# The high parts of the summed weights: kept in on-chip memory, or streamed from DRAM with the low parts

## The reference

```python
scale = cond @ norm_w.T + 1.0
ms = jnp.mean(x * x, axis=-1, keepdims=True)
h = x * (scale[:, None, :] * jax.lax.rsqrt(ms + EPS))
u = h @ up_w.T
val, gate = jnp.split(u, 2, axis=-1)
h = val * jax.nn.gelu(gate, approximate=False)
hq = act_quant(h)          # int8 steps by the row's largest value
wq = weight_quant(down_w)  # -1, 0, 1 by the mean of all
y = hq @ wq.T
return y + x
```

## Time and profile before

| | us |
|---|---|
| median of 3 runs | 759.24 (759.22 to 759.32) |
| the profiled execution's own time | 759.19 |
| its span in the trace | 757.4 |
| PE busy | 737.0 (97%) |
| DVE busy | 546.7 (72%) |
| ACT busy | 345.7 (46%) |
| POOL busy | 98.9 (13%) |
| DMA | 116.63 MB, mean 154 GB/s |

### The profile page before, as it was taken

The page is one execution under the profiler, slowest core; times in us unless marked ns, Lnnn a source line. Parts: engine busy times, 40 slices in busy tenths (PEclk is TensorE's granted clock), DMA queues, the critical chain, the costliest instruction groups (busy, mean ns, idle before and its releaser), DMA issues.

```text
span 757.4 us, 15715 instructions
## 1 busy us (share of the span) xinstructions
PE 737.0 (97%) x6218; PEld 610.5 (81%) x6218; DVE 546.7 (72%) x1066; ACT 345.7 (46%) x674; POOL 98.9 (13%) x137
## 2 busy tenths in 40 slices
PE   3999999999999999999999999999999999999998
PEld 2888889888578887888778887788878887688864
DVE  5467777888788775878667775777758776377747
ACT  5789756443254432553235442444325342233425
POOL 2211376763413000000000000000000000000000
PEclk9999999999999999999999999999999999999999
DMA  9877673756645444343533434343443333453302
GB/s 324 285 259 241 189 264 123 229 178 223 200 135 183 153 153 148 116 140 99 183 117 116 130 116 163 108 152 122 125 160 103 98 98 117 128 170 98 103 29 84
DMA packets 43929, 116.63 MB, mean 154 GB/s; under 512 B 4944, under 2 KB 5200, under 8 KB 42704
## 3 DMA queue, kind: packets, MB, share of 16 engines
q1 hardware_dynamic: 43856, 115.63, 47.6%
HBM read 98.83 MB, written 16.78 MB: 153 GB/s over the span
## 4 chain that ended last, share of the span: by engine, by line
PE 86%; DVE 5%; ACT 3%; issue 3%; DMA 1%; POOL 0%; SPq 0%; DVEq 0%; ACTq 0%
PE ps_v L525 16%; PE ps_v L526 15%; PE ps_v L527 15%; PE ps_y L626 12%; PE ps_g L526 8%; PE ps_g L525 8%; PE ps_g L527 8%; PE ps_v L690 1%; DMA sums<-in_up_t_dram 1%; DMA h<-in_x_rows_dram 1%; ACT g L733 1%; ACT w_hi L776 1%; DVE h L1053 0%; PE ps_m L609 0%; DVE xt L1004 0%
## 5 line engine op out<-in xcount | busy, mean ns | idle before, releaser
L525 PE MATMUL ps_v<-x_hi,w_hi 128*128 128x256 f16 x1216 | 332.0, 273 | 3.3 <-DVE ps_g L1036 1.3
L527 PE MATMUL ps_v<-x_hi,w_lo 128*128 128x256 f16 x1216 | 331.9, 273 | 0.0
L526 PE MATMUL ps_v<-x_lo,w_hi 128*128 128x256 f16 x1216 | 331.9, 273 | 0.0
L526 PE MATMUL ps_g<-x_lo,w_hi 128*128 128x256 f16 x640 | 174.8, 273 | 0.0
L527 PE MATMUL ps_g<-x_hi,w_lo 128*128 128x256 f16 x640 | 174.8, 273 | 0.0
L525 PE MATMUL ps_g<-x_hi,w_hi 128*128 128x256 f16 x640 | 174.8, 273 | 0.0
L715 ACT COPY ps_g<-ps_v 128x256 f32<-128x256 f32 x96 | 34.3, 357 | 230.7 <-PE ps_v L527 230.7
L525 PEld LDWEIGHTS ps_v<-x_hi,w_hi 128*128 128x128 f16 x1216 | 119.1, 98 | 21.4 <-DVE ps_g L1036 2.7
L526 PEld LDWEIGHTS ps_v<-x_lo,w_hi 128*128 128x128 f16 x1216 | 119.1, 98 | 15.7
L527 PEld LDWEIGHTS ps_v<-x_hi,w_lo 128*128 128x128 f16 x1216 | 119.1, 98 | 13.9
L726 ACT ACTIVATE g<-ps_g,w_unscale 128x512 f32<-128x512 f32 x128 | 87.3, 682 | 68.1 <-PE ps_g L527 68.0
(11 more groups left out here) (113 smaller groups left out, 581.7 us busy)
## 6 DMA issues: line engine op xcount, KB each, us to landing
w_lo<-w_lo_dram SPq DMA_DIRECT2D x96, 448.0 KB, 3.3
q<-in_up_t_dram SPq DMA_DIRECT2D x16, 512.0 KB, 5.1
xt<-in_x_cols_dram SPq DMA_DIRECT2D x8, 1024.0 KB, 5.2
res<-in_x_rows_dram SPq DMA_DIRECT2D x26, 256.0 KB, 3.6
out_dram<-res SPq DMA_DIRECT2D x26, 256.0 KB, 2.9
sums<-in_up_t_dram SPq DMA_DIRECT2D x12, 512.0 KB, 4.7
xs<-in_x_rows_dram SPq DMA_DIRECT2D x22, 256.0 KB, 3.8
w_lo_dram<-w_lo SPq DMA_DIRECT2D x16, 256.0 KB, 4.8
```

The source lines that it names most:

```text
L525: pe.matmul(to, w_hi[:, wh:wh + P], hi, start=start and kt == 0, stop=False, skip_group_check=True)
L526: pe.matmul(to, w_hi[:, wh:wh + P], lo, start=False, stop=False, skip_group_check=True)
L527: last = pe.matmul(to, w_lo[:, wl:wl + P], hi, start=False, stop=(kt == 1), skip_group_check=True)
```

## The change

The high parts of the four summed operands no longer stay in `w_hi`. ACT writes the high part beside the low part into an output tile of 2048 fp16 a partition (`sum_tile`: for even k the new tile `sum_out`, for odd k both halves of `xs`), DVE writes the low part before it, and one store takes both to DRAM: 512 KB for each of 16 sums instead of 256 KB. `WL` grows from 2048 to 3072, so each slot of `w_lo` and each row of `w_lo_dram` holds four loaded low parts, four summed low parts and four summed high parts; the load of a tile from n = 32 on brings 2816 fp16 a partition, 704 KB instead of 448 KB. In `product` a summed operand's high part comes from the slot. `w_hi` keeps the high parts of the loaded operands alone, with no overlap between tiles.

With this the waits move. ACT's `sum_high` no longer waits for PE (`val_ready`) but, from k = 2 on, until the store of sum k - 2 has landed; DVE's `sum_low` loses that wait. PE's `first_pair` loses its wait for `ws_ready`. A sum's weights in places 2 and 3 now lie in the slot of that number in one piece of 1024 float32, where they lay in two pieces of 512 in a pair of slots.

```diff
@@ -59,10 +60,9 @@
     HB = TB // 2
     TT = TB // P
     WJ = 2 * KT * P
-    WO = NOP * 2 * P
     WA = 4 * 2 * P
     WS = 4 * 2 * P
-    WL = WA + WS
+    WL = WA + 2 * WS
     PAD = 2 * P
     XO = NOP * 2 * HB
     PER_B = NB // B
@@ -134,8 +133,7 @@
 
         lo_dram = nc.dram_tensor("w_lo_dram", [J, P, WL], FP16, kind="Internal").ap()
 
-
-        w_hi = sb("w_hi", [P, PAD + J * WO], FP16)
+        w_hi = sb("w_hi", [P, J * WA], FP16)
         w_lo = sb("w_lo", [P, LS * WL], FP16)
         w_unscale = sb("w_unscale", [P, J], F32)
         dw = sb("dw", [P, J * D], BF16)
@@ -143,6 +141,7 @@
 
         xt = sb("xt", [P, KT, TB], F32)
         xs = sb("xs", [P, 2, D], F32)
+        sum_out = sb("sum_out", [P, 2 * WS], FP16)
         res = sb("res", [P, 2, D], F32)
         ta = sb("ta", [P, 2, HB], F32)
         tb = sb("tb", [P, 2, HB], F32)
@@ -322,15 +321,14 @@
 
         def wb(j):
 
-            return PAD + j * WO
+            return j * WA + PAD
 
         def sum_raw(k):
 
             place = SUM_PLACE[k]
             if place < 2:
-                return sums[:, place * WS:(place + 1) * WS].rearrange("p (a n) -> p a n", a=2)
-            slots = w_lo[:].bitcast(F32).rearrange("p (s c) -> p s c", s=LS)
-            return slots[:, 2 * place - 4:2 * place - 2, WA // 2:WL // 2]
+                return sums[:, place * WS:(place + 1) * WS]
+            return w_lo[:, place * WL + WA:(place + 1) * WL].bitcast(F32)
 
         def sum_loads(k):
 
@@ -338,7 +336,7 @@
 
         def sum_tile(k):
 
-            return xs[:, k % 2, :].bitcast(FP16)
+            return sum_out[:] if k % 2 == 0 else xs[:].rearrange("p a n -> p (a n)").bitcast(FP16)
 
         def sum_store(k):
 
@@ -363,7 +361,7 @@
                     sp.wait_ge(ws_ready, user + 1)
                 elif SUM_PLACE[k] < 2:
                     sp.wait_ge(dw_ready, J)
-                sp.dma_start(sum_raw(k), up_t[k].rearrange("p (a n) -> p a n", a=2)).then_inc(sum_loaded[SUM_PLACE[k]], 16)
+                sp.dma_start(sum_raw(k), up_t[k]).then_inc(sum_loaded[SUM_PLACE[k]], 16)
 
             def store_sum(k):
                 stored, _ = sum_store(k)
@@ -378,8 +376,8 @@
                     sp.wait_ge(lo_stored[j % LS], 16 * (j // LS + 1))
                 if in_seven(n):
                     if n < 2 * J + LS:
-                        last = max(k for k in range(J) if SUM_PLACE[k] == 2 + (n % LS) // 2)
-                        sp.wait_ge(ws_ready, last + 1)
+                        if n % LS in (2, 3):
+                            sp.wait_ge(ws_ready, max(k for k in range(J) if SUM_PLACE[k] == n % LS) + 1)
                     if n < 3 * J:
                         stored, count = sum_store(j)
                         sp.wait_ge(stored, count)
@@ -397,7 +395,7 @@
                 if t >= 2:
                     sp.wait_ge(sumsq_ready, TT + t + 1)
                 if c == 4 and i < 2:
-                    stored, count = sum_store(J - 2 + t % 2)
+                    stored, count = sum_store(J - 1)
                     sp.wait_ge(stored, count)
                 sp.dma_start(xs[:, t % 2, :], x_rows[c][:, i * D:(i + 1) * D]).then_inc(xs_loaded[t % 2], 16)
 
@@ -518,12 +516,16 @@
                     pe.wait_ge(x_lo_ready, made_at(b, xop))
                 to = bank[:, half * HB:(half + 1) * HB]
                 for kt in range(2):
-                    wh = wb(j) + (op * 2 + kt) * P
                     wl = (n % LS) * WL + PAD + (op * 2 + kt) * P
+                    if op >= OS3:
+                        w = w_lo[:, wl + WS:wl + WS + P]
+                    else:
+                        wh = wb(j) + (op * 2 + kt) * P
+                        w = w_hi[:, wh:wh + P]
                     xa = x_at(b, xop) + kt * HB
                     hi, lo = x_hi[:, xa:xa + HB], x_lo[:, xa:xa + HB]
-                    pe.matmul(to, w_hi[:, wh:wh + P], hi, start=start and kt == 0, stop=False, skip_group_check=True)
-                    pe.matmul(to, w_hi[:, wh:wh + P], lo, start=False, stop=False, skip_group_check=True)
+                    pe.matmul(to, w, hi, start=start and kt == 0, stop=False, skip_group_check=True)
+                    pe.matmul(to, w, lo, start=False, stop=False, skip_group_check=True)
                     last = pe.matmul(to, w_lo[:, wl:wl + P], hi, start=False, stop=(kt == 1), skip_group_check=True)
                 return last
 
@@ -556,8 +558,6 @@
 
             def first_pair(n):
                 pe.wait_ge(lo_loaded[n % LS], 16 * ((n - J) // LS + 1))
-                if n < 3 * J:
-                    pe.wait_ge(ws_ready, n % J + 1)
                 if n >= NV:
                     pe.wait_ge(h_ready, n - NV + 1)
                 bank = ps_v[:, n % NV, :]
@@ -778,8 +778,12 @@
 
             def sum_high(k):
                 act.wait_ge(s_step, 4 * (k + 1))
-                act.wait_ge(val_ready, J + min(k + 2, J))
-                act.activation(w_hi[:, wb(k) + WA - PAD:wb(k) + WO].rearrange("p (a n) -> p a n", a=2), sum_raw(k), ACT.Copy,
+                if k >= 2:
+                    stored, count = sum_store(k - 2)
+                    act.wait_ge(stored, count)
+                if k == 1:
+                    act.wait_ge(sumsq_ready, 3 * TT)
+                act.activation(sum_tile(k)[:, WS:2 * WS], sum_raw(k), ACT.Copy,
                                scale=w_scale[:, k:k + 1]).then_inc(ws_hi_ready, 1)
 
             def sum_down(k):
@@ -867,7 +871,7 @@
             pool.tensor_copy(ident_top, ident[:]).then_inc(ident_ready, 1)
 
             def sum_weights(k):
-                a21, a22, a11, a12 = [sum_raw(k)[:, i // 2, (i % 2) * 2 * P:(i % 2 + 1) * 2 * P] for i in range(4)]
+                a21, a22, a11, a12 = [sum_raw(k)[:, i * 2 * P:(i + 1) * 2 * P] for i in range(4)]
                 pool.wait_ge(sum_loaded[SUM_PLACE[k]], sum_loads(k) * 16)
                 pool.tensor_tensor(a22, a21, a22, ALU.add).then_inc(s_step, 1)
                 pool.wait_ge(s_step, 4 * k + 1)
@@ -958,13 +962,8 @@
 
             def sum_low(k):
                 dve.wait_ge(ws_hi_ready, k + 1)
-                dve.wait_ge(sumsq_ready, 3 * TT)
-                if k >= 2:
-                    stored, count = sum_store(k - 2)
-                    dve.wait_ge(stored, count)
-                dve.scalar_tensor_tensor(out=sum_tile(k).rearrange("p (a n) -> p a n", a=2), in0=sum_raw(k),
-                                         scalar=w_scale[:, k:k + 1],
-                                         in1=w_hi[:, wb(k) + WA - PAD:wb(k) + WO].rearrange("p (a n) -> p a n", a=2),
+                dve.scalar_tensor_tensor(out=sum_tile(k)[:, 0:WS], in0=sum_raw(k), scalar=w_scale[:, k:k + 1],
+                                         in1=sum_tile(k)[:, WS:2 * WS],
                                          op0=ALU.mult, op1=ALU.subtract).then_inc(ws_ready, 1)
 
             def rsqrt(c):
```

## The result

| | before | after |
|---|---|---|
| median | 759.53 us (758.05 to 761.25, 20 runs) | 763.27 us (760.68 to 766.81, 20 runs) |
| profiled execution | 759.19 us, span 757.4 | 764.99 us, span 763.2 |
| mean granted clock, all executions | 0.999 or more | 0.9985 or more in 11, 0.995 to 0.998 in 9 |

The changed kernel is slower: the ratio is 1.0048, with a 95% interval from 1.0036 to 1.0061. The forecast of 760.4 us and its range up to 762.2 were too low. The 20 executions fall in two groups. The 11 with the full clock have a median of 761.79 us, the 9 with a lower one 764.44.

A forecast was written before the change was run, and what follows sets the result against it. PE, busy 97%, was taken as the bound, except where a DMA, POOL, ACT and DVE decide near 224 to 240 us. +1.5 for the late load and -0.25 gave +1.25 on 759.19: 760.4 us, range 759.0 to 762.2.

The forecast's parts named there:

- the load of the fifteenth sum: Sum weights' load near 224 us, behind 512 KB more in its queue: 1.5 us later, bounds 0.8 to 3.2.
- rival B: Added bytes almost free, or POOL's steps quicker with less DVE beside them (0.3 us): 759.0 to 759.6; chance 0.22.
- Rival C: Fifteenth sum's load also waits for the store ahead to be written to DRAM: up to 3.2 us late, 762.2; chance 0.15.
- the steady part: Block windows with larger operand loads and stores: traffic does not brake PE and loads arrive in time, 0 us.
- ACT's new wait: ACT's `sum_high` for k waiting for the store of k - 2: tightest pair 2 us early, 0 us.
- PE's other source: PE's matmuls reading a summed high part from `w_lo` rather than `w_hi`: same shape, 0 us.
- The sixteenth sum: Next sum, from POOL at 241.2 to ACT at 242.45: slack covers a load 1.5 us late, 0 us.
- rival D: Operand loads late in every block, PE stopping at each block's start: 765 us or later; chance 0.04.
- the small gain: Near 205 us POOL comes later and mostly misses DVE's `sum_low`, so `turn_max` waits less: -0.25 us (0 to -0.27).

The follow-up runs named there:

- e5: Changed kernel with 448 KB operand loads from n = 36 on and 256 KB sum stores from k = 4 on; 761.02 us, ratio 1.0020.
- e6: Changed kernel with 448 KB operand loads from n = 36 on, its 512 KB sum stores kept; 761.56 us, ratio 1.0024.
- e10: Changed kernel with only DVE's rsqrt chain for block 3 moved one iteration later, loads as late as before; 763.13 us, ratio 1.0044.
- e4: Changed kernel with the loads for sums issued ahead of the stores of sums in each SP iteration; 761.57 us, ratio 1.0022.
- e2: Kernel before with the fifteenth sum's weights loaded one iteration earlier; 758.68 us, ratio 0.9985.
- e3: Kernel before with the fifteenth sum's load issued later, behind its iteration's operand load, no byte added; 762.23 us, ratio 1.0036.
- e1: Changed kernel with the fifteenth sum's weights loaded one iteration earlier; 761.32 us, ratio 1.0025.
- e7: Changed kernel with the loads for the fifteenth and sixteenth sums one iteration earlier; 760.46 us, ratio 1.0006.
- e8: Kernel before with the loads for the fifteenth and sixteenth sums and the rsqrt chain moved, loads one iteration earlier, chain one later; 759.08 us, ratio 0.9986.

## Why the prediction was wrong

**Two terms of the sum failed: "the load of the fifteenth sum", by its size, and the granted clock, which the sum left out.** With the pause as measured and the clock at its full level the time is 761.79 us, the median of those 11 executions, still inside the range of 759.0 to 762.2. What takes the median to 763.27 is the clock.

**The load.** Place and chain were right: the load near 224 us, then POOL, ACT, DVE, PE, with nothing later to give the time back. The load was priced 1.5 us longer and came 2.87 us longer. The price for 256 KB came from two means, one of how the operand loads' own landing grows with their size and one of the whole queue, and gave 0.8 us for each of the two additions. For the store that was about right, 0.67 us (e5 to e6). For the operand loads it was 2.05 us (e6 to after), two and a half times the price. Each of these is from one execution a kernel, though e10's load, with the bytes of after, took 8.29 us. Of the 2.05 us the operand load ahead shows 1.1 in its own landing (5.9 us against 4.8). The sum reckoned only with bytes ahead in the queue; the operand load issued behind the sum's load, 3.70 us later and in flight with it, grew too. That it makes up the rest is possible and not shown. The prediction's upper bound for the term was 3.2 us.

PE's pause was to be 2.4 us instead of 0.86. It was 2.99. So 2.13 of the 2.87 us reached PE, where the prediction passed all of the load's delay on. SP issued the load 1.10 us later than before, with PE 1.40 us later there, and POOL's four steps took 3.20 us instead of 3.48. The second is what rival B had named, with 0.3 us.

**Rival C had the better price, and its mechanism is not shown.** It forecast a load up to 3.2 us late and 762.2 us, because the store ahead has to be written out first. With the order turned round the load takes 1.6 us less (e4), but that is what the forecast's own price gives for 512 KB, and 256 KB more in the store cost 0.67 us, less than that price. Most of the addition came from the operand loads, which C did not name. The Trainium skill ("DMA: Bandwidth & Descriptors", Queues, rings and completion order) has a semaphore write land after earlier writes of its engine. The landings agree: in after those of the operand load, the store, the sum's load and the next operand load come in the order of issue, at 230.2, 231.2, 233.6 and 235.1 us. The landings give no price for it. By another rule of the Trainium skill (same page, Anatomy of one DMA), fitted there to DMAs issued from GpSimd and not from SP, the 512 KB would cost an estimated 1.2 us; the runs show 2.87.

**Missed altogether: the granted clock.** The sum treated a pause as lost time at its own length. In the profiled execution it also cost half the clock for some 6 us behind it, and 9 of 20 executions have a lowered mean clock. The groups' medians are 764.44 and 761.79 us, 2.65 apart; the profile has 2.7 us of slow matmuls, less the 0.45 of the gap that went. Of the 2.9 us between the forecast and 763.27, 1.5 is the way from the full-clock median to the median of all. The full-clock median itself is 2.26 above before: 2.13 for the pause, -0.27 for `turn_max`, and 0.4 left, which block 1 would explain.

**Missed as well: block 1.** I looked for ACT's waits for POOL and found two; I did not look at how far DVE stood behind PE near 180 us, where its chain leaves no slack. DVE in after runs later against PE there. L665 on PE is 0.70 us later than before in this execution:

```profile
77.15 0.32 PE L665 MATMUL ps_y<-ident,d_sum 128*128 128x128 f32 x1 [0.68 <-DVE d_sum L1186]
```

```profile
77.85 0.32 PE L665 MATMUL ps_y<-ident,d_sum 128*128 128x128 f32 x1 [0.68 <-DVE d_sum L1185]
```

The `hidden` of DVE that stood at 163.65 stands at 165.35 in after, 1.70 later, so 1.0 us has been added. At 129.17 it was 1.14 later (128.03 before), and the first 512 KB store is issued at 133.6. So 0.44 us of this was there before any added byte moved. The other 0.56 came in the stretch of sums. There POOL waits 0.92 us for a load at 142.11, and ACT 0.77 us for POOL at 146.80. The trace of before has neither wait; e2's, with the bytes of before, has one of 0.82 us of POOL at 139.95 but none of ACT there.

```profile
128.03 0.74 DVE L1053 SCALAR_TENSOR_TENSOR h<-ps_v,w_unscale,g 128x512 f32<-128x512 f32 x1
163.65 0.74 DVE L1053 SCALAR_TENSOR_TENSOR h<-ps_v,w_unscale,g 128x512 f32<-128x512 f32 x1
```

```profile
129.17 0.74 DVE L1052 SCALAR_TENSOR_TENSOR h<-ps_v,w_unscale,g 128x512 f32<-128x512 f32 x1
142.11 0.94 POOL L876 TENSOR_TENSOR w_lo<-w_lo 128x256 f32<-128x256 f32 x1 [0.92 <-DMA w_lo<-in_up_t_dram]
146.80 1.15 ACT L786 ACTIVATE xs<-w_lo,w_scale 128x1024 f16<-128x1024 f32 x1 [0.77 <-POOL w_lo L882]
165.35 0.74 DVE L1052 SCALAR_TENSOR_TENSOR h<-ps_v,w_unscale,g 128x512 f32<-128x512 f32 x1
```

Over the kernels with the chain in its old place the gap is 0, 0.41 and 0.64 us with the bytes of before, and 0.84 to 2.22 with those of after (0.89 in e5 and e6). It follows DVE: counted from L665 on PE, that `hidden` stands 0.56 and 0.66 us later than before in e2 and e3 (gaps 0.41 and 0.64), 1.0 in after (0.97), 1.54 in e1 (1.53) and 2.24 in e7 (2.22). But in e1 and e7, which have the largest gaps, 1.6 and 1.8 us of this stand already at the `hidden` ahead of the first larger store. This is e7's:

```profile
130.79 0.74 DVE L1052 SCALAR_TENSOR_TENSOR h<-ps_v,w_unscale,g 128x512 f32<-128x512 f32 x1
```

From there to the later `hidden` e7 adds 0.5 us and e1 nothing. So the larger stores and loads can have made some 0.5 us of the gap, in seven of the eight traces of the changed kernel and its variants; e2 adds 0.4 without them. No run changed the bytes in that stretch alone. The rest is a spread between executions, of which the last section names a source.

**Right:** the steady part at 0 (88.81 us of PE in 89.00, DMA share 0.53 where 0.55 was forecast, operand loads at a median of 4.3 us where 4.1 was forecast). ACT's new wait at 0: in after ACT was never released by a store, though the stores took 5.2 to 5.4 us at the median (in e4, with the stores behind the loads, it was once, for 0.72 us). PE's other source at 0. The sixteenth sum was covered in after, and was not where PE came earlier (e1). No rival D: no wait of PE for an operand load shows (its one wait for a DMA, 3.9 us at the start, is in before too).

**Right in part by luck: the small gain.** The gap ahead of `turn_max` went from 1.32 to 1.05 us, since `sum_low` took 1.28 us at 206.11 with POOL idle until 207.00, as said. All eight traces of the changed kernel and its variants have 1.05. But the kernel before does not always meet POOL there: e2 and e3, whose edits come later, have 1.06 and 1.09, and e8 1.28.

```profile
208.48 0.63 PE L609 MATMUL ps_m<-ident,h_max 128*128 128x128 f32 x4 [1.06 <-issue]
```

**Two slips of arithmetic** changed nothing: 96 times 256 KB are 25.2 MB in the units used elsewhere, not 24.6; and B's terms, 0.8 - 0.25 - 0.3, give 759.4 us, not 759.6.

## What to carry to other kernels

Price bytes added to a queue at the transfer on which an engine chain without slack waits, with those issued behind it that are in flight with it, and not by the mean rate; here the added 29 MB cost nothing in the last two thirds of the run and, in the profiled execution, 4.4 us at one load (2.13 for the pause and 2.25 for the clock). Then ask what a pause of PE does to its clock: here, in the profiled execution, 2.1 us more of pause brought 2.7 us of slow matmuls with it. When one transfer sets the end of a chain, issue it an iteration earlier before judging a change that adds traffic, and look what the next one of its kind then does.

## What the runs showed of the hardware

- **The clock after a pause.** Two gaps of 1.94 and 1.05 us, with 0.8 us of work between them, were followed by a granted clock of 0.50 for some 6 us. Over the kernels, with both gaps and the executions with a lowered clock: 1.94 + 1.05 (after, 9 of 20), 1.84 + 1.05 (e10, 5 of 5), 1.61 + 1.05 (e3, 3 of 8, the traced one at full clock); 0.19 + 1.05 (e4, 0 of 8), 0.23 + 1.05 (e6, 0 of 11), 0.86 (before, 0 of 20). One gap of 2.22 us near 180 us was followed by it too (e7, 1 of 12). e1 (2 of 11) and e5 (1 of 11) have such executions without a trace of them; the largest gaps in their traces, past the start, are 1.53 and 1.05 us. The same kernel does it in some executions and not in others. Whether their pauses differed is not known, and no run tells why.
- **Slow matmuls at the start.** In every profile PE's first 128x256 matmuls, from 15.5 to 16.7 us on, are as slow as those behind the pause, 0.42 us each and 0.21 us apart, though the granted clock of these windows reads 1.00 in before and after. The last slow one starts between 18.50 us (e6) and 20.87 us (e4), without order by kernel: 19.04 in before, 20.83 in after. DVE's L965 stood 0.34 us earlier in after than in before at 19.4 us, and 0.72 later at 25.0 (25.73), so the 0.70 us by which the two profiles differ at 77 us came in that stretch.
- **Small DVE operations beside POOL.** The 128x4 operations of the chain take 0.16 us, or 0.57 for many of those that begin while a POOL operation runs; in the 128x1024 `sum_low` it is 1.28 against 1.75. Which of them meet depends on shifts of a few tenths of a us, so a small delay on one engine can come out as 0.4 to 0.5 us more or less on the other. This is a source of the spread in block 1: near 121 us, before any added byte moved, two of DVE's 128x512 operations in a row take 0.69 and 1.10 us in before, and 1.10 and 1.09 in after.
